# Quantised FFN: GpSimd multiplies the second pair of tiles by its block scales, and the results are written before the first silu product

## What is computed

```python
def fake_quant_nvfp4(x, global_scale):
    xb = x.reshape(sh[:-1] + (sh[-1] // BLOCK, BLOCK))          # BLOCK = 16
    amax = jnp.max(jnp.abs(xb), axis=-1, keepdims=True)
    sc = jnp.clip(amax / FP4_MAX * global_scale, 0.0, FP8_MAX)
    dq = sc.astype(jnp.float8_e4m3fn).astype(jnp.float32) / global_scale
    a = jnp.clip(jnp.abs(xb) / safe_dq, 0.0, FP4_MAX)
    q = jnp.sign(xb) * _FP4_VALS[jnp.digitize(a, _FP4_MIDS)]
    return (q * dq).reshape(sh)

gate_out = nvfp4_linear(x, gate_w, s_in[0])      # quantises x and w, then multiplies
up_out = nvfp4_linear(x, up_w, s_in[0])
hidden = jax.nn.silu(gate_out) * up_out          # 1024 inner units
return nvfp4_linear(hidden, down_w, s_in_down[0])
```

## Time and profile before

| | us |
|---|---|
| Median of 3 runs | 822.29 (822.2 to 826.0) |
| Profiled execution, own time | 821.41 |
| Its span | 819.7 |
| VectorE busy | 622.8 (76%) |
| TensorE busy | 629.9 (77%) |
| ScalarE busy | 413.8 (50%) |
| GpSimd busy | 211.4 (26%) |

### The profile page before, as it was taken

The page is one execution under the profiler, slowest core; times in us unless marked ns, Lnnn a source line. Parts: engine busy times, 40 slices in busy tenths (PEclk is TensorE's granted clock), DMA queues, the critical chain, the costliest instruction groups (busy, mean ns, idle before and its releaser), DMA issues.

```text
span 819.7 us, 14039 instructions
## 1 busy us (share of the span) xinstructions
PE 629.9 (77%) x3935; PEld 460.6 (56%) x3944; DVE 622.8 (76%) x1538; ACT 413.8 (50%) x696; POOL 211.4 (26%) x259
## 2 busy tenths in 40 slices
PE   6499891699999996689999999983535675567564
PEld 3387671377667764578788888872113343234333
DVE  5288888866566654868988889873489899999994
ACT  1333331232333332545557667555647877687664
POOL 6537754255544554001121222110000000000000
PEclk9699996799999999898999999998657887887797
DMA  8885553621112101500000000000000000000001
GB/s 322 275 298 201 196 182 104 220 70 54 54 59 73 58 21 51 180 1 1 0 0 0 0 0 0 1 1 4 1 1 0 26 13 13 26 26 13 13 26 52
DMA packets 30956, 53.98 MB, mean 66 GB/s; under 512 B 4973, under 2 KB 23806, under 8 KB 29760
## 3 DMA queue, kind: packets, MB, share of 16 engines
q1 hardware_dynamic: 24768, 39.29, 14.4%
q0 software_dynamic: 5568, 13.61, 4.8%
q10 hardware_dynamic: 576, 0.55, 0.2%
HBM read 39.38 MB, written 15.93 MB: 67 GB/s over the span
## 4 chain that ended last, share of the span: by engine, by line
DVE 22%; PE 21%; issue 8%; ACT 7%; DVEq 1%; POOL 0%; ACTq 0%; DMA 0%; POOLq 0%
PE bank L1260 4%; PE quad L1244 3%; DVE hh L2144 3%; PE bank L1275 2%; PE bank L1457 2%; DVE ctxs L2095 2%; DVE nS L1917 2%; DVE nM L1922 2%; ACT x L924 2%; DVE ctxs L2083 2%; DVE nS L1925 2%; PE quad L1235 1%; PE quad L1425 1%; PE quad L1434 1%; DVE x L2117 1%
## 5 line engine op out<-in xcount | busy, mean ns | idle before, releaser
L1457 PE MATMUL bank<-dT,hqT 128*128 128x256 bf16 x256 | 54.0, 383 | 44.4 <-ACT hqT L970 44.4
L1123 PE MATMUL quad<-W1s,xts 128*128 x160 | 74.2, 603 | 0.7 <-DVE hid L1741 0.7
L1140 PE MATMUL bank<-W2s,hidT 128*128 x320 | 72.5, 379 | 0.3 <-ACT hidT L716 0.3
L1140 PEld LDWEIGHTS bank<-W2s,hidT 128*128 128x128 f32 x320 | 60.0, 190 | 12.6 <-issue 5.3
L605 POOL TENSOR_TENSOR X<-fo,X 128x256 f32<-128x256 f32 (+1 forms) x32 | 21.9, 685 | 166.4 <-DVE fo L1939 152.7
L1457 PEld LDWEIGHTS bank<-dT,hqT 128*128 128x128 bf16 x256 | 32.6, 135 | 56.6 <-ACT hqT L970 46.7
L712 ACT ACTIVATE hid<-hid 128x512 f32<-128x512 f32 x40 | 25.3, 633 | 75.2 <-DVE hid L1741 75.2
L1260 PE MATMUL bank<-nVB,nPT 128*128 128x34 f32 x512 | 63.0, 279 | 0.0
L1260 PEld LDWEIGHTS bank<-nVB,nPT 128*128 128x128 f32 x512 | 59.6, 191 | 3.7
L545 POOL DMA_INDIRECT x_after_ffn<-row,niU x40 | 39.5, 986 | 70.3 <-DVE row L1753 52.8
L2144 DVE SCALAR_TENSOR_TENSOR hh<-quad,gmx,sil 128x512 f32<-128x512 f32 x64 | 45.1, 745 | 13.0 <-PE quad L1434 9.6
(11 more groups left out here) (324 smaller groups left out, 1515.5 us busy)
## 6 DMA issues: line engine op xcount, KB each, us to landing
row<-rows_by_expert SPq DMA_DIRECT2D x40, 134.0 KB, 2.1
W1s<-in_ctxO SPq DMA_DIRECT2D x4, 1024.0 KB, 7.9
ctxs<-in_ctxT SPq DMA_DIRECT2D x4, 1024.0 KB, 14.5
W1s<-in_W SPq DMA_DIRECT2D x8, 512.0 KB, 3.8
W2s<-in_W SPq DMA_DIRECT2D x8, 512.0 KB, 4.7
out<-yo SPq DMA_DIRECT2D x16, 256.0 KB, 2.1
X<-x_after_ffn SPq DMA_DIRECT2D x7, 516.0 KB, 6.9
b1s<-in_b SPq DMA_DIRECT2D x1, 2048.0 KB, 8.0
```

The source lines that it names most:

```text
L1123: ins = pe.matmul(bank[2 + u % 2][:], xt[:, u, c, :], W1s[:, bass.ds(ex, 1), c, :].rearrange("p o s -> p (o s)"), start=c == 0, stop=c == ...
L1140: ins = pe.matmul(bank[6 + u % 2][:, 0:D], hidT[:, u % 2, c, :], W2s[:, bass.ds(ex, 1), c, :].rearrange("p o s -> p (o s)"), start=c == 0, ...
L1457: ins = pe.matmul(bank[(1, 7)[u // 2]][:, (u % 2) * D:(u % 2 + 1) * D], hqT[:, u % 2, c, :], dT[:, c, :], start=c == 0, stop=c == FT - 1)
```

## The change

GpSimd gets a loop over the eight groups. It waits for `s_iv`, a new signal that VectorE gives when the block scales are ready, and for `s_fh` of the group before, and multiplies `hh[1]` by its inverse scales into `wraw[:, 1]`; it signals `s_vp`. VectorE's `hidden_scaled(1)` is gone, from the loop and from the last group. ScalarE's `hidden_half(1)` waits for `s_vp`, and in ScalarE's order it moves from in front of silu 0 to behind silu 1. In VectorE's order both `results` stand in front of `product(t, 0)`; before, one stood between the clamp of the second pair and `product(t + 1, 1)`, the other behind `product(t + 3, 3)`. The clamp of the second pair moves from in front of `product(t + 1, 1)` to behind it. Three semaphore names of one attention branch now share those of the other branch, of which only one runs.

```diff
@@ semaphores
-        n_cn, n_cT, n_cTe, n_wo, n_fin = [sem(n) for n in ("n_cn", "n_cT", "n_cTe", "n_wo", "n_fin")]
+        n_cn, n_cT, n_cTe = s_cn, s_cT, s_cTe
+        n_wo, n_fin = [sem(n) for n in ("n_wo", "n_fin")]
+        s_iv, s_vp = sem("s_iv"), sem("s_vp")
@@ GpSimd
+            for g in range(NTILE // 4):
+                pool.wait_ge(s_iv, g + 1)
+                if g:
+                    pool.wait_ge(s_fh, 2 * g)
+                pool.sem_inc(s_idle, 1)
+                inv = inv4[:, NBX + NBH // 2:NBX + NBH].rearrange("p (t b) -> p t b", t=2)
+                pool.tensor_tensor(wraw[:, 1, :].rearrange("p (t k b) -> p t k b", t=2, k=BLOCK),
+                                   hh[1][:].rearrange("p (t k b) -> p t k b", t=2, k=BLOCK),
+                                   inv.unsqueeze(2).broadcast_to([P, 2, BLOCK, inv.shape[2]]), ALU.mult).then_inc(s_vp, 1)
@@ ScalarE
             def hidden_half(g, p):
-                act.wait_ge(s_vh, g * 2 + (p + 1))
+                act.wait_ge((s_vh, s_vp)[p], g + 1)
                 act.mul(hf[p][:], top(wraw[:, p, :]), ABOVE).then_inc(s_fh, 1)
...
                 x_out(i + 1)
-                hidden_half(i, 1)
                 silu(t, 0)
                 silu(t + 1, 1)
+                hidden_half(i, 1)
                 hidden_size(t, 0)
@@ VectorE, group
                 block_scales(slice(0, NBX + NBH))
+                v.sem_inc(s_iv, 1)
                 rows_scaled()
                 hidden_scaled(0)
                 rows_quantised(g + 1)
-                hidden_scaled(1)
                 v.wait_ge(s_fh, g * 2 + 1)
...
                 hidden_quantised(0)
+                if later:
+                    results(g - 1)
                 product(t, 0)
+                product(t + 1, 1)
                 v.wait_ge(s_fh, g * 2 + 2)
                 clamped(hf[1][:])
-                if later:
-                    results(g - 1, (0,))
-                product(t + 1, 1)
                 rounded(hf[1][:])
                 product(t + 2, 2)
                 hidden_quantised(1)
                 product(t + 3, 3)
-                if later:
-                    results(g - 1, (1,))
@@ VectorE, last group
             block_scales(hid_c)
-            for p in range(2):
-                hidden_scaled(p)
+            v.sem_inc(s_iv, 1)
+            hidden_scaled(0)
             results(g - 1)
```

## The result

The changed kernel takes 861.58 us (858.47 to 863.32, four runs), the kernel before 823.98 us with its fourth run. The ratio is 1.045, with a 95% interval from 1.040 to 1.050: slower, by 37.6 us, against a forecast of 855.4 us. The profiled execution took 863.32 us, 41.9 more than that of before.

The account below looks back on a forecast made before the run. TensorE's down products were taken to bind a group's first half, VectorE the second. GpSimd's contention gave 6 x 4.6 + 5.5 = +33.1 us, so 822.29 goes to 855.4 us, range 823 to 866.

Parts of the forecast that it names:

- VectorE's removed 2.28 us: `hidden_scaled(1)`, taken from VectorE in each group's first half, where TensorE's down products were said to set the pace.
- The order's own cost: New order of results, products and `hidden_half(1)`: 0.4 us longer a group even with an undisturbing GpSimd, +2.8 over seven groups.
- the second half: From product 0 to the end of product 3: 9.8 us forecast against 9.11 before, so 0.7 more.
- The signal on VectorE: The added signal to GpSimd that the block scales are ready, put at 0 to 0.1 us a group.
- GpSimd's product, 4.67 us from rows 5: GpSimd's 128x2048 float32 product, 4.67 us, extrapolated from traced 128x256 (0.613 us) and 128x1024 (2.351 us) products.
- Who gets the port, and when: Behind the reciprocal: `rows_scaled` first, then GpSimd from 715.6 to 720.3, then `hidden_scaled(0)`, 4.8 us late.
- The removed work counting in full: Rival: VectorE sets the pace throughout, each group loses up to 2.28 us, kernel 806 us; chance 0.08.
- Fast forms alone waiting: Rival: GpSimd runs beside two-input products, only the rows' clamp waits 1.5 us; 0.9 a group, 828.6 us; chance 0.22.
- VectorE keeping the port while work is queued: Rival: GpSimd gets in only when VectorE waits for `hidden_half(0)`; +2.1 us a group, 837 us; chance 0.12.
- The size: Whole forecast cost: 4.6 us for each of six groups plus 5.5 for the first, +33.1 us.
- the way from the fourth down product's end to product 0: End of the first half, through gate and up: 723.03 to about 724.5, moved later as one block.
- the first group: No down products in front, so it takes all 4.8 us of lateness and the 0.7: +5.5 us.

Follow-up runs that it names:

- e1: The changed kernel, but GpSimd only signals and multiplies nothing, second pair's scaled values left out; against the kernel before: ratio 1.006 (845.56 against 840.05 us).
- e9_beside_before: The kernel before in its own order, with a GpSimd product of the same shape on unneeded tiles added; ratio 1.044, stretch 275.5 us.
- e4: The complete changed kernel, but VectorE signals GpSimd only behind `hidden_quantised(0)`; ratio 1.015 to the kernel before, stretch 250.1 us.

## Why the prediction was right

- **VectorE's removed 2.28 us lie in a half that it doesn't bound.** Right: without a neighbour the seven groups take 198.0 us with the 2.28 us removed and 197.8 with them kept, and moving only the copies frees product 0.
- **The order's own cost, 0.4 us a group.** Right in its mechanism, too large in size: the idle of 0.8 in front of the second clamp stands as worked out; that in front of product 1 is 0.3 to 0.5 where I had 0.6. In `e1` the second half grows by 0.36 where I had 0.7, and product 0 gains 0.2 on average where I had 0.3, which leaves 0.1 a group. That the sum still came to +2.4 for +2.8 is luck: the first group alone gave 1.4. In the changed kernel products 0 to 3 take 9.63 us, 9.8 in the working, 9.11 before. The signal on VectorE, put at 0 to 0.1 us, costs 0.12 (`rows_scaled` starts 2.31 behind the reciprocal's start instead of 2.19).
- **GpSimd's product, 4.67 us from rows 5.** It measures 4.54 beside VectorE's PSUM work and 4.36 between two VectorE instructions. The figure of the Trainium skill ("GPSIMD Engine Reference", section 3.1), 4497 ns, is nearer.
- **Who gets the port, and when.** Right: `rows_scaled` first, GpSimd between it and `hidden_scaled(0)`. The latter ends 4.4 us late (10.06 us behind the reciprocal's start, 5.61 before) where I had 4.8. The rule of the Trainium skill ("SBUF — State Buffer", section "Who interferes with whom"), that two SBUF inputs contend with a GpSimd read and not with a write, agrees with all three runs: 6.60 us beside a product, 3.98 beside a copy, 2.28 beside a memset.
- **The rivals.** The removed work counting in full is out (`e1`: no gain). Fast forms alone waiting is out: it is a two-input product that shows 6.60 us. The memset lengthens only the fast clamp, by 0.1 us, and its stretch is 243.2, no more than that of the same order without GpSimd's work (245.1). VectorE keeping the port while work is queued is out: GpSimd came in between two instructions 0.09 us apart in overlap.
- **The size: +36.1 in the stretch against +33.1, +37.1 in the seven groups.** The term that was too small is the way from the fourth down product's end to product 0. I moved it as a block of 1.5 us (723.03 to 724.5). TensorE's rows in the same group:

```profile
748.57 1.03 PE L1427 MATMUL bank<-identb,xq 128*128 128x128 bf16 x8 [3.23 <-DVE xq L2143]
749.89 1.89 PE L1468 MATMUL bank<-dT,hqT 128*128 128x256 bf16 x8 [0.28 <-ACT hqT L981]
752.00 1.48 PE L1436 MATMUL quad<-gT,xqT 128*128 128x512 bf16 x3 [0.22 <-issue]
753.28 1.64 PE L1445 MATMUL quad<-uT,xqT 128*128 128x512 bf16 x4
754.75 1.03 PE L1436 MATMUL quad<-gT,xqT 128*128 128x512 bf16 x4
```

The fourth down product ends at 751.78, 4.0 us later in its group than before. From there to product 0 it takes 2.66 us instead of 1.77. The up product's four matmuls took 1.03 us before and 1.64 here, the next gate's 1.03: their first part fits the lower of the two clock levels (1.2 GHz). The granted clock from 750.0 to 755.5 is 0.59, against 0.74 from 721.0 to 725.5 before; over the whole group it is 0.70 against 0.74. So 4.0 + 0.9 in the first half and 0.5 in the second make the 5.4 us of this group; I had 3.9 and 0.7.

That this way is longer by the clock is shown by other groups. Windows from the fourth down product's end to product 0, two groups of the changed kernel:

```profile
652.22:653.63 1.41, 1.35 (x7) 0.65 (x7) 1.19 (x3) 0.86 (x2) 0.00 (x0) 1.00 0.05 12
785.71:788.37 2.66, 2.44 (x6) 0.91 (x6) 1.18 (x2) 1.38 (x2) 0.00 (x0) 0.50 0.39 134
```

And two of `e9_beside_before`, where no transfer runs at that place:

```profile
712.45:713.94 1.49, 1.49 (x8) 0.58 (x6) 1.46 (x2) 1.49 (x3) 0.00 (x0) 0.99 0.00 0
679.04:681.70 2.66, 2.66 (x7) 0.91 (x6) 1.49 (x2) 2.25 (x3) 0.00 (x0) 0.50 0.00 0
```

With a granted clock of 1.00 (2.4 GHz) the way takes 1.4 to 1.5 us, as in the working; at 0.50 (1.2 GHz) it takes 2.66, with transfers or without. In the changed kernel's six groups with down products it takes 1.41, 2.21, 2.60, 2.66, 2.66 and 2.67. What brings the clock down there stays open. Behind an idle of 3.23 us, in which TensorE waited for xq, the group above has the low clock, but the group with 1.41 us has the same idle, 3.24, in the same place.

Over these six groups, product 0 starts 17.2 us behind the reciprocal's start on average where I had 16.5, though the down product ends 0.2 earlier than worked out: 4.3 us in all. Another 1.7 come from the choice of the group: I read the one in which product 0 starts latest (12.60), and the average before is 12.3. The second half, 9.6 for 9.8, and the first group, 5.0 for 5.5, take 1.9 back, and what is left of the 4.0 (37.1 less 33.1) is rounding.

## What to carry to other kernels

Before work goes from VectorE to GpSimd, look at what VectorE does at that moment: a product with both inputs in SBUF did not run beside a GpSimd instruction that reads SBUF in this layer in any of the runs, so the slower engine's whole time landed on VectorE's path. A fast single-input form was held a little even by a GpSimd write (0.53 us for 0.42); no run has one beside a GpSimd read in this layer. Products that read PSUM and one SBUF tile ran beside it undisturbed (`e4`). And a busy share of 91% doesn't say that removed work is worth its time; the wait in front of the next shared step does, and moving a single instruction there filled it (27.6 us a group for 27.8 to 28.5). Read that wait in more than one group: here it ran from nothing to 0.67 us.

## What the runs showed of the hardware that was not expected

- An instruction that waits for the port shows the wait as its own busy time, which the prediction had left open: `hidden_scaled(0)` at 6.60 us, GpSimd's product at 5.49 with 4.36 of work. Busy shares grow without work.
- GpSimd got the port between two VectorE instructions that overlap by about 0.09 us in the trace, each time: seven of seven in the change, seven of seven beside the kernel before, seven of seven with the copy.
- The last group differs: GpSimd's product there shows 6.56 us and `hidden_scaled(0)` 2.29. With no `rows_scaled` in front, VectorE's product went first, and GpSimd waited for it: its row ends 4.38 us behind VectorE's.
